# The end of a two-layer graph network: stores on two queues, work moved to GpSimd and ScalarE, TensorE's branch taken twice

## The reference, cut to what matters

```python
edge_index = stack([src, dst])                       # 40000 edges, 1250 nodes
h = maximum(layernorm(x), 0)
x = x + L0(h)        # messages by 32 relations from 8 bases, summed by dst, + bias
h = maximum(layernorm(x), 0)
x = x + L1(h)
...
def L1(x):           # D = 512
    deg = counts of row (with self loops);  dis = rsqrt(deg)
    h = x @ W.T + b
    out = segment_sum((dis[row] * dis[col])[:, None] * h[row], col)
    return relu(out)
```

## Time and profile before

| | us |
|---|---|
| median of 3 runs | 593.65 |
| lowest and highest run | 590.59, 594.0 |
| the profiled execution, its own time | 594.36 |
| its span, first to last instruction | 592.6 |
| TensorE busy | 497.5 (84%) |
| VectorE busy | 345.0 (58%) |
| GpSimd busy | 354.1 (60%) |
| ScalarE busy | 155.3 (26%) |
| mean granted TensorE clock | 0.922 of full speed |

### The profile page before, as it was taken

How to read it: one execution, slowest core, us unless ns; L and a number is a source line. 1 busy time by engine, 2 the same in 40 slices (tenths; PEclk the granted TensorE clock), 3 DMA queues, 4 the chain that set the end, 5 groups by cost and what they waited for, 6 DMA issues and landing times.

```text
span 592.6 us, 16039 instructions
## 1 busy us (share of the span) xinstructions
PE 497.5 (84%) x5873; PEld 318.2 (54%) x5873; DVE 345.0 (58%) x999; ACT 155.3 (26%) x280; POOL 354.1 (60%) x476
## 2 busy tenths in 40 slices
PE   3140667899999899999999998998989998999973
PEld 1020655555666556666656665655656565665530
DVE  8994674577855356857766765654566324242036
ACT  3682552364202122212320320320233101131020
POOL 3535657367776776766757767767767777730000
PEclk9665667899999999999999999998989999999995
DMA  8798969566787887886866968878967888845006
GB/s 275 248 358 287 369 213 335 178 175 176 209 259 216 258 259 206 256 254 173 276 208 178 281 181 231 276 207 243 270 204 227 261 239 253 241 147 160 0 21 156
DMA packets 51861, 132.84 MB, mean 224 GB/s; under 512 B 11775, under 2 KB 17776, under 8 KB 51702
## 3 DMA queue, kind: packets, MB, share of 16 engines
q0 software_dynamic: 27040, 99.60, 55.6%
q1 hardware_dynamic: 23788, 30.99, 16.7%
q10 hardware_dynamic: 954, 1.13, 0.6%
HBM read 123.14 MB, written 11.10 MB: 227 GB/s over the span
## 4 chain that ended last, share of the span: by engine, by line
PE 70%; DVE 11%; DMA 9%; issue 4%; ACT 2%; POOL 1%; SPq 1%; DVEq 0%; ACTq 0%
PE PS L1754 28%; PE PS L1722 21%; DMA gath<-rows_layer,srcs 7%; PE PS L1795 7%; PE PS L1746 5%; PE PS L1774 4%; DMA types_by_slot<-h_t 1%; PE PS L1730 1%; POOL gath L805 1%; PE PS L1589 1%; DVE room_b L1558 1%; PE PS L1763 1%; DVE gath L1572 1%; DVE stats L1076 1%; ACT room_b L951 1%
## 5 line engine op out<-in xcount | busy, mean ns | idle before, releaser
L805 POOL DMA_INDIRECT gath<-rows_layer,srcs x335 | 334.3, 998 | 154.7 <-PE PS L1730 83.3
L1722 PE MATMUL PS<-sel,gath 128*128 128x48 f16 (+7 forms) x4020 | 303.3, 205 | 28.8 <-issue 12.0
L1722 PEld LDWEIGHTS PS<-sel,gath 128*128 128x128 f16 x4020 | 241.8, 102 | 154.8 <-issue 64.5
L1754 PE MATMUL PS<-room_b,zt 128*128 128x512 f16 x384 | 127.7, 383 | 0.4 <-issue 0.3
L1754 PE MATMUL PS<-room_b 128*128 128x512 f16 (+1 forms) x384 | 117.1, 382 | 0.5 <-DMA gath<-rows_layer,srcs 0.4
L1730 PE MATMUL PS<-oh_ad,gath 128*128 128x30 bf16 (+7 forms) x335 | 64.6, 193 | 1.9 <-DVE c_i L1369 1.9
L1795 PE MATMUL PS<-u_t,room_c 128*128 128x512 f16 (+2 forms) x200 | 57.1, 395 | 6.3 <-issue 3.8
L874 ACT CAST val<-val_f 128x64 f16<-128x64 f32 x42 | 11.0, 262 | 176.9 <-DVE val_f L1246 176.9
L1277 DVE TENSOR_TENSOR masks<-iota_n,dloc 128x24 bf16<-128x24 f32 (+12 forms) x92 | 18.0, 196 | 62.5 <-issue 33.2
L1754 PEld LDWEIGHTS PS<-room_b 128*128 128x128 f16 (+1 forms) x384 | 38.4, 105 | 12.9 <-DMA gath<-rows_layer,srcs 0.5
L1283 DVE TENSOR_TENSOR sel<-masks,val 128x192 f32<-128x192 bf16 (+12 forms) x92 | 38.6, 420 | 0.0
(11 more groups left out here) (245 smaller groups left out, 505.3 us busy)
## 6 DMA issues: line engine op xcount, KB each, us to landing
room_b<-in_L_gnn_bases_dram SPq DMA_DIRECT2D x8, 1024.0 KB, 11.0
gath<-rows_layer,srcs POOLq DMA_INDIRECT x335
x_base<-in_x_dram SPq DMA_DIRECT2D x5, 500.0 KB, 5.5
x_t<-x_base SPq DMA_DIRECT2D x19, 128.0 KB
u_t<-in_x_dram SPq DMA_DIRECT2D x9, 256.0 KB, 6.0
types<-types_by_slot SPq DMA_DIRECT2D x144, 16.0 KB
x_layer<-x_t SPq DMA_DIRECT2D x18, 128.0 KB, 4.2
gath<-x_layer SPq DMA_DIRECT2D x18, 128.0 KB, 2.7
```

The lines of the kernel that those rows point to most:

```text
L805: pool.indirect_dma_start(out=gath[:, s % UN, :], out_offset=None, in_=tab0_d[:, :], in_offset=bass.IndirectOffsetOnAxis(ap=srcs[:, s:s + ...
L1722: last = mm(there, gath[:, s % UN, D * t + P * f:D * t + P * (f + 1)], sel_parts[:, here, k, 0:NB * w, u], start=first and t == 0 and u == ...
L1754: last = mm(PS[0:r, PBANK[q], :], zt[q][:, t, f, b, 0:r], base_hl[:, b, u, f, :], start=(m == 0), stop=(m == NM - 1))
```

## The change

Four things, all in the last 20 us. (1) Each block's first half is stored by SyncE's queue and its second by ScalarE's. (2) For the blocks t = 0, 1, 3 and 6 (`PTAIL`) the addition of x1 is done by GpSimd, which raises a new semaphore `s_resp`; the stores wait for `s_resp` or `s_res` by block. (3) For t = 3 and 6 the maximum with 0 is a separate instruction on ScalarE. (4) TensorE spreads the high parts of blocks 0 to 7 first, jumps over one branch that holds the matmuls of all eight, spreads their low parts, and does the same for blocks 8 and 9. The first spread waits for the high part of u only (`s_uhi`), the low parts for `s_uev`. Blocks 8 and 9 get an `out_tmp` of their own.

```diff
+    PTAIL = [0, 1, 3, 6]
...
+        def store(eng, t, half):
+            if t in PTAIL:
+                eng.wait_ge(s_resp, PTAIL.index(t) + 1)
+            else:
+                eng.wait_ge(s_res, t + 1 - sum(p < t for p in PTAIL))
+            d, n, p = halves(TAIL[t])[half]
+            eng.dma_start(out[d:d + n, :], final(TAIL[t])[p:p + n, :]).then_inc(s_out, 16)
...
-            for t, i in enumerate(TAIL):
-                sp.wait_ge(s_res, t + 1)
-                for d, n, p in halves(i):
-                    sp.dma_start(out[d:d + n, :], final(i)[p:p + n, :]).then_inc(s_out, 16)
+            for t in range(NT):
+                store(sp, t, 0)
...
+            pool.wait_ge(s_back, 32 * QL)
+            for n, t in enumerate(PTAIL):
+                x1 = final(TAIL[t])[0:ROWS[TAIL[t]], :]
+                pool.wait_ge(s_relu, n + 1)
+                g.tensor_tensor(x1, out_tmp(t)[0:ROWS[TAIL[t]], :], x1, ALU.add).then_inc(s_resp, 1)
...
+            sent = 0
+            for t in PTAIL[2:]:
+                while sent < t - 2:
+                    store(act, sent, 1)
+                    sent += 1
+                act.wait_ge(s_sum, t - 1)
+                there = out_tmp(t)[0:ROWS[TAIL[t]], :]
+                a.activation(there, there, ACT.Relu).then_inc(s_relu, 1)
+            for t in range(sent, NT):
+                store(act, t, 1)
...
-            add_x1(0)
-            add_x1(1)
-            add_begun(2)
-            for t in range(3, NT):
-                add_begun(t)
-                add_x1(t - 1)
-            add_x1(NT - 1)
+            dve.wait_ge(s_back, 32 * QL)
+            add_begun(2)
+            for t in range(3, NT):
+                add_begun(t)
+                if t - 1 not in PTAIL:
+                    larger(t - 1)
+            larger(NT - 1)
...
+            for group in (range(0, 8), range(8, NT)):
+                for n in group:
+                    if n == 0:
+                        pe.wait_ge(s_uhi, NT)
+                    elif n == 6:
+                        pe.wait_ge(s_ub, NT)
+                    elif n == 7:
+                        pe.wait_ge(s_x1, NT)
+                    elif n >= 8:
+                        pe.wait_ge(s_relu, n - 7)
+                    spread(TAIL[n], QL, 0, C, FBANK[n], n >= 2 and n - 2 not in late)
                 with pe.If(any_order > 0):
                     pe.wait_ge(s_cext, 32)
+                    pe.wait_ge(s_uev, NT)
+                    for n in group:
+                        for q in range(NT):
+                            for t in range(2):
+                                for k in range(2):
+                                    spread(TAIL[n], q, t, k, FBANK[n], False)
+                if 0 in group:
+                    pe.wait_ge(s_uev, NT)
+                for n in group:
+                    spread(TAIL[n], QL, 1, C, FBANK[n], False).then_inc(s_fin, 1)
```

More of the change, by code:

```diff
@@ L530, in gnn_kernel @@
         s_res = sem("s_res")
+        s_resp = sem("s_resp")
         s_out = sem("s_out")
@@ L590, in out_tmp @@
         def out_tmp(i):
-            return room_b[:, D * (i % 8):D * (i % 8 + 1)]
+            return room_b[:, D * (i if i < 8 else i + 26):D * ((i if i < 8 else i + 26) + 1)]
         cext = room_b[:, FT * NB * D // 4:FT * NB * D // 4 + NT * N].bitcast(f16).rearrange(
@@ L1559, in add_begun, with larger @@
                                        ALU.mult, ALU.add).then_inc(s_sum, 1)
-            def add_x1(t):
+            def larger(t):
                 j = TAIL[t]
[L1563 to L1572, removed]
-            add_x1(0)
-            add_x1(1)
+                x1 = final(j)[0:ROWS[j], :]
+                dve.wait_ge(s_sum, t - 1)
+                v.scalar_tensor_tensor(x1, out_tmp(t)[0:ROWS[j], :], 0.0, x1, ALU.max, ALU.add).then_inc(s_res, 1)
+            dve.wait_ge(s_back, 32 * QL)
             add_begun(2)
```

## The result

| | us |
|---|---|
| changed kernel, median of 8 runs | 587.86 (584.8 to 592.38) |
| kernel before, median of 8 runs | 591.38 (590.59 to 594.0) |
| ratio | 0.9942, 95% interval 0.992 to 0.9965 |
| profiled execution, its own time / span | 592.38 / 590.5 |
| mean granted TensorE clock | 0.932 (0.922 before) |

The change makes the kernel 0.6% faster: inside the band of 1% that the prediction called "same", but with an interval that leaves 1 out. The time lies outside the predicted range (589.0 to 595.2).

A forecast was written before the change was run, and what follows sets the result against it. The prediction took the stores, 3.0 us behind VectorE, to bound the end. VectorE's end +1.0, backlog -3.0 and last block +0.15 shortened the span by 1.8 us; from the 593.65 us median that gave 591.8 us, range 589.0 to 595.2.

The forecast's parts named there:

- The level it started from: Whole kernel before: median 593.65 us, from which the predicted shortening was taken to give 591.8 us.
- the cases: Forecast (0.50) and its rivals for the last stretch; the range over them was 589.0 to 595.2 us.
- The move: Last 20 us: the span shortens by 1.8 us, from 592.6 to 590.8 us.
- VectorE's end: VectorE's last addition: ends at 587.85 us instead of 586.85, +1.0 us.
- backlog of the stores: Output stores at the end: their 3.0 us lag behind VectorE disappears with two queues.
- behind the last issue: From last store issue to span's end: 2.78 us plus about 0.15 for the shared last block.
- the first jump: TensorE's branch over 320 matmuls: reached about 573.6 us, costs 2.8 us, TensorE resumes at 576.4.
- Exclusion between GpSimd and VectorE: x1 additions: GpSimd's and VectorE's instructions with two SBUF operands exclude each other; one VectorE addition is held 1.0 us.
- The rival that the halves share what limits them: Final stores: two queues together move no more than one; time 594.3 us, chance 0.30.
- The sum by that figure: Final stores with the skill's 6% gain: 12.0 us become 11.3, time about 593.3 us.
- The far jump: TensorE's two final branches: each costs 6.24 us, time 597.9 us, chance 0.10.
- The cheap jump: TensorE's two final branches: each costs 0.21 us, time about 588.5 us, chance 0.05.

The follow-up runs named there:

- branch_twice: Kernel before with only TensorE's edit, high parts first and the branch taken twice instead of ten times: 592.03 us, ratio 1.0011.
- stores_and_branch: Kernel before with stores on two queues and TensorE's branch taken twice, all x1 additions on VectorE: 589.27 us, ratio 0.9977.
- jump_early: Changed kernel with TensorE's first branch moved right behind the last projection, three branches in all: 586.02 us, ratio 0.9915 to the kernel before.
- gpsimd_three: Changed kernel with the first branch moved early, and block 1's x1 addition given back to VectorE: 586.01 us, ratio 0.9905 to the kernel before.
- stores_two_queues: Kernel before with one edit, each block's second half stored by ScalarE's queue: 588.94 us, ratio 0.9963.
- again: Changed kernel run once more, unchanged, beside the kernel before: 587.94 us, ratio 0.9957.

## Why the prediction was wrong, step by step

**The level it started from: wrong, the largest error.** "The median of the runs is 593.65. Taken from that, 591.8 us." Three runs stood behind it, 590.59, 593.65 and 594.0; eight gave 591.38. That is 2.3 of the 3.9 us between 591.8 and 587.86. The forecast's own move was -1.85 us; from 591.38 it would have read 589.5. The range was built from the cases and the spread of the *before* runs, with nothing for the error of a median of three whose runs span 3.4 us, nor for the changed kernel's own spread (584.8 to 592.38). Set down by the 2.3 us, its range is 586.7 to 592.9 and holds the result.

**The move: right in sign and cause, too small.** Measured 2.7 us by the tails, 2.1 by the two profiles that start at the same 572.07, 3.5 by the medians (interval of the ratio: 2.1 to 4.7 us). Term by term, on the means of the two profiles of each kernel:

| term of the sum | predicted | measured |
|---|---|---|
| VectorE's end | +1.0 | -0.15 (14.9 to 14.75 us of the tail) |
| backlog of the stores | -3.0 | -3.3 (3.0 and 3.7 to 0) |
| behind the last issue | +0.15 | +0.7 (2.8 and 2.7 to 3.4 and 3.5) |

**VectorE's end: the term of the move that failed.** I had TensorE reach the first jump at 573.6 ("one matmul early"), stop until 576.4, spread at 0.42 us, and stop a second time for 2.9 us, so that block 8 came at 583.9 and VectorE waited for it. The trace shows the branch reached at 572.1, with eight spreads still to run: its sequencer stands far ahead of the matmuls. The jump itself was longer (3.83 us, 3.35 in the second profile), and the two errors nearly cancel: TensorE resumes at 575.99. But the clock was then still at 1.00, where in the earlier trace rows, behind a stop of nearly the same length, it was falling: ten spreads took 2.33 us instead of 4.2. That goes with the branch edit (2.33 us for ten in branch_twice and stores_and_branch too, 2.74 for six in the four profiles with ten branches made for this study). With the edit TensorE stands idle 1.66 us before its first spreads of the end, without it 2.44; which of the differences keeps the clock up the runs don't show. And the second jump took 1.39 us, so blocks 8 and 9 were there by 579.8, four us earlier than VectorE needed them. VectorE started at 576.92 (predicted 577.85), never waited, and was bound by its own work: 10.1 us, the 8.9 of the sum and 1.1 from being held back by GpSimd. Why a jump over 80 matmuls costs 1.3 to 1.4 us here and 2.7 to 2.9 in jump_early isn't settled.

**Exclusion between GpSimd and VectorE: right in size, one block off.** "The second addition then holds back VectorE's first x1 addition by 1.0 us." It was the second x1 addition, held 1.0 us (1.67 for 0.68), by GpSimd's third; GpSimd's second itself took 1.73 instead of 1.27. By the Trainium skill (SBUF — State Buffer, "Who interferes with whom") a VectorE instruction whose other input is in PSUM does not contend; the trace agrees: two such additions take 1.40 us beside GpSimd (578.99) and 1.41 in branch_twice, where GpSimd does nothing (575.06). gpsimd_three shows the price by removing it.

**The stores: right in size, not for the reason given.** The backlog went as forecast: I took 300 GB/s for a pair of halves; 288 was read in the changed kernel and 285 in jump_early, and the last issue stood at VectorE's end. The rival that the halves share what limits them falls: its sign was a last issue over 1.5 us behind VectorE. For it spoke the DMA engines' share of 0.9 at 204 GB/s; that share did not mean that no more could be moved (0.92 at 288). But both it and my reading ("a 64-row transfer cannot keep the 16 DMA engines at speed and that a pair covering all partitions can, at least half way") took 204 GB/s for a limit of the transfers. The rows above show it as the pace of one engine's issues, and stores_two_queues lost the backlog at 210 GB/s. That the forecast of this term came out is in part luck. The Trainium skill (SBUF — State Buffer, "Can I just issue two DMAs to hit both halves?") has two concurrent transfers, at partitions 0 and 64, only 6% ahead of one. The sum by that figure started from the same 12.0 us and falls with them. 288 against 204 to 219 GB/s is 32 to 41% more, but here the one queue was held back by its issues, so no run measures what the page compares.

**Behind the last issue: too small.** I had 0.15 us for the last block's two halves landing together. With two queues the end came 3.4 to 3.5 us behind the last issues instead of 2.7 to 2.8, in stores_two_queues 3.4 behind ScalarE's.

**The other rivals.** The far jump at 6.24 us fell: 3.83 was the longest. The cheap jump at 0.21 us fell too (1.34, in `again`, was the shortest of the change); its time, 588.5, was the nearest only because the level was 2.3 us too high.

**The parts.** That GpSimd's and TensorE's parts buy nothing at VectorE's end was predicted for GpSimd's ("The removed work buys nothing") and holds for both: alone they measure 1.001 and 1.0011.

## What to carry to other kernels

When the last store is issued well behind the last result, look first at how often one engine can issue. Here it was every 0.64 us, so 128 KB a store came to 205 GB/s, and a DMA share of 0.9 was not the limit; a second issuing engine took the backlog away. A branch that is always jumped over can cost microseconds, depending on where it stands; where its engine waited for data anyway, one of 3.78 us cost nothing. And a median of three runs is no level: take its error into the range before anything else.

## What the runs showed of the hardware that I had not expected

TensorE's sequencer reaches a branch well before the matmuls ahead of it have run (572.1 us, with eight spreads queued until 573.99), so a jump hides behind queued matmuls as well as in a wait: in jump_early one of 1.95 us, reached at 568.7, left no gap in eighteen spreads.

Single DMA issues stretch from 0.5 or 0.6 to between 1.2 and 2.0 us in nearly every profile (1.36, 1.79, 1.17, 2.01), on SyncE's queue or, in stores_two_queues, on ScalarE's:

```profile
L1027 ACTq DMA_DIRECT2D out_dram<-gath x9: 497/507/1375, 572.2 to 584.3; - x9
```

In twelve of the thirteen profiles the longest of these issues overlaps a packet of the queue of kind "instruction" (57 packets in all in the changed kernel's profile), of which only three or four fall into the last 20 us; in the profile of before the two packets start at 581.3 and 584.6, the two long issues at 581.24 and 584.57. The exception is stores_and_branch, whose longest issue takes 1.05 us. Whether the one causes the other was not tried.
